# A token tower on one core: six gathered heads and two dense ones, replaced by eight dense heads

## The reference, cut to what matters

```
q = (x @ Wq).reshape(b, n, 8, 64) / 8
sim = einsum(x @ Wq_pk, pk_keys)              # 2 halves x 8 heads x 64 keys
scores, idx = top_k(sim, 16)                  # of each half
final, pk_idx = top_k(scores0[i] + scores1[j], 16)
kv_scores = softmax(final); ind = idx0 + 64 * idx1 + 4096 * head
k = sum over the 16 picks of kv_scores * keys_table[ind]
v = sum over the 16 picks of kv_scores * values_table[ind]
out = causal softmax(q k^T) v, heads joined, @ Wo
```

## Time and profile before

| what | value |
|---|---|
| median of 2 runs | 8935.81 us (8913.85 to 8957.77) |
| span of the profiled execution | 8919.9 us |
| granted TensorE clock, mean | 0.660 |
| PE, PEld busy | 65%, 43% |
| DVE, ACT, POOL busy | 36%, 23%, 49% |
| software DMA (the gathers) | 144384 packets, 295.20 MB |

### The profile page before, as it was taken

How to read it: one execution, slowest core, us unless ns; L and a number is a source line. 1 busy time by engine, 2 the same in 40 slices (tenths; PEclk the granted TensorE clock), 3 DMA queues, 4 the chain that set the end, 5 groups by cost and what they waited for, 6 DMA issues and landing times.

```text
span 8919.9 us, 86784 instructions
## 1 busy us (share of the span) xinstructions
PE 5811.1 (65%) x23616; PEld 3849.5 (43%) x23616; DVE 3250.8 (36%) x14095; ACT 2088.5 (23%) x4517; POOL 4374.7 (49%) x4574
## 2 busy tenths in 40 slices
PE   1367576575766757676665767667576666757677
PEld 1244444353444534444443544445344443534443
DVE  4334242433423243342424334232433423243036
ACT  0112122121322213132221312222131222222143
POOL 3454545545454554545455454545545445554500
PEclk9567566666756667675666667566666756666577
DMA  1111111111111111111111111111111111111100
GB/s 41 51 41 32 39 34 37 44 31 39 30 40 35 39 41 32 41 31 41 35 38 42 32 40 32 39 35 40 40 31 39 33 36 38 39 36 32 41 12 14
DMA packets 166480, 321.90 MB, mean 36 GB/s; under 512 B 82044, under 2 KB 90836, under 8 KB 165774
## 3 DMA queue, kind: packets, MB, share of 16 engines
q0 software_dynamic: 144384, 295.20, 12.5%
q1 hardware_dynamic: 21230, 20.00, 0.8%
q10 hardware_dynamic: 288, 0.07, 0.0%
HBM read 310.37 MB, written 4.61 MB: 35 GB/s over the span
## 4 chain that ended last, share of the span: by engine, by line
PE 36%; another core or an unknown queue 25%; issue 20%; DVE 14%; ACT 5%; DVEq 0%; ACTq 0%; DMA 0%; SPq 0%
PE gath L615 7%; PE accu L477 5%; PE dense L469 4%; PE work L668 2%; PE dense L464 2%; PE sims L662 2%; ACT past L902 2%; PE dense L470 1%; PE work L643 1%; PE work L698 1%; PE work L544 1%; PE work L655 1%; DVE front L1244 1%; DVE i L1243 1%
## 5 line engine op out<-in xcount | busy, mean ns | idle before, releaser
L429 POOL DMA_INDIRECT store<-in,idx_now x4512 | 4358.2, 966 | 3970.7 <-PE gath L615 2195.0
L615 PEld LDWEIGHTS gath<-wbd,store 128*128 128x128 f32 (+1 forms) x9024 | 1607.2, 266 | 783.7 <-issue 747.5
L615 PE MATMUL gath<-wbd,store 128*128 128x8 f32 (+1 forms) x9024 | 1553.7, 304 | 551.5 <-issue 432.8
L469 PE MATMUL dense<-parts_f,hot 128*128 128x375 bf16 x3072 | 905.0, 416 | 495.3 <-issue 420.7
L477 PE MATMUL accu<-dense_w,store 128*128 128x375 f32 x2048 | 1123.8, 640 | 11.9 <-issue 10.1
L902 ACT ACTIVATE past<-dense,edge 128x375 bf16<-128x375 f32 x1024 | 587.0, 573 | 2176.3 <-remote 1338.9
L464 PE MATMUL dense<-ranksT,hot 128*128 128x375 bf16 x1008 | 407.8, 405 | 847.1 <-ACT past L902 678.7
L469 PEld LDWEIGHTS dense<-parts_f,hot 128*128 128x128 bf16 x3072 | 322.2, 114 | 894.0 <-issue 820.6
L910 ACT ACTIVATE dense_w<-dense 128x375 f32<-128x375 f32 x1024 | 493.8, 482 | 887.3 <-remote 547.3
L464 PEld LDWEIGHTS dense<-ranksT,hot 128*128 128x128 bf16 x1008 | 158.4, 157 | 1083.0 <-issue 1033.7
L477 PEld LDWEIGHTS accu<-dense_w,store 128*128 128x128 f32 x2048 | 500.1, 258 | 142.2 <-issue 107.6
(11 more groups left out here) (285 smaller groups left out, 6983.9 us busy)
## 6 DMA issues: line engine op xcount, KB each, us to landing
store<-in,idx_now POOLq DMA_INDIRECT x4512
x_in<-in SPq DMA_DIRECT2D x16, 187.5 KB
store<-in SPq DMA_DIRECT2D x1, 2048.0 KB, 8.7
queries_kept<-n3T SPq DMA_DIRECT2D x16, 93.8 KB
h_saved<-h SPq DMA_DIRECT2D x16, 93.8 KB
store<-queries_kept SPq DMA_DIRECT2D x16, 93.8 KB, 2.4
store<-h_saved SPq DMA_DIRECT2D x16, 93.8 KB
out<-store SPq DMA_DIRECT2D x16, 93.8 KB
```

Of the source, the lines that this page charges most:

```text
L429: nc.gpsimd.indirect_dma_start(rows[0:slots, r * PER + i, :], None, kv_table, bass.IndirectOffsetOnAxis(ap=idx_now[0:slots, at:at + 1], ax ...
L469: mm(dense[:, 1, 0:S], hot[:, c, :], parts[:, k, h, :], start=(k == 0), stop=False)
L615: last = mm(gath[:, 0, at:at + 8], rows[0:slots, r * PER + i, :], wbd[0:slots, t * GATHERS + n, :], start=True, stop=True)
```

## The change

All eight heads are dense, and no step needs a gather. The weight of a row (i0, i1) is a product of two factors: exp of key i0's score against the maximum (`firsts`), and the same for i1 over the sum (`seconds`, as three bf16 parts, 32 of the 64 keys a group). What is new or different:

- A batch has 256 steps in 260 slots. The slot j holds, on TensorE: spread(j-2) (the constant `spread` brings the second factor to the 128 rows, `far` subtracts 1024 past), in every second of the first 56 slots one of the factors of a later head, accu(j-4), and coded(j) once past(j-1) is there. One PSUM bank holds `coded`, two take spreads and factors in turn; an item waits until the one two before it is taken.
- Of spread(i) with i even, ScalarE makes the Relu `shown` and GpSimd multiplies it by the first factor (`weigh` on GpSimd). With i odd VectorE does both in one instruction out of PSUM (`weigh` on VectorE), in its own stream between picks.
- The tables are streamed each batch: 32 pieces of 512 KB in a ring of 4, on SP's queue, ahead of that batch's `keep` and load of x.
- VectorE's picks lose row numbers, `places`, and the candidate indices; the codes are made for 8 heads by products and reductions over 2048 elements, the run comparison over 2048 too, and there are a difference over 1024 and the parts of the second factor. A tile has 23 pieces.
- Attention takes 88 slots (`STEPS_A`, `STEPS_B`: 14 or 15 a head for six heads, none for the last two), and the value matmuls of the last three heads move into its heads 4 to 6.

```diff
-FILL_FIRST = ((5, 2), (3, 2))
-FILL_SECOND = ((11, 6), (7, 4))
-FIRST_HEAD, STEPS_A, STEPS_B = 2, (1, 1, 1, 1, 1, 1, 0, 0), (2, 2, 2, 2, 2, 2, 0, 0)
+STEPS = H * CHUNKS
+SPREAD_LAG, SUM_LAG = 2, 4
+PREPARED_EVERY = 2
+FILL_PREPARE = (4, 3, 3, 3, 4, 4, 4, 4, 3)
+FILL_GRADIENT = (6, 6, 6, 6, 6)
+PICKS_GRADIENT = (2, 2, 1, 1, 1)
+FILL_FIRST = (8, 32)
+FILL_SECOND = (36, 34)
+FIRST_HEAD, STEPS_A, STEPS_B = 2, (8, 8, 8, 8, 8, 8, 0, 0), (6, 6, 6, 6, 7, 7, 0, 0)
+PICKS_INSIDE = (3, 3, 3, 3, 3, 3, 1, 1)
+PIECES_A, PIECES_B = 9, 14
+BY_VECTOR = frozenset(range(1, STEPS, 2))
...
+            def load_pieces(b):
+                for n in range(PIECES):
+                    sp.wait_ge(s["piece_out"], b * PIECES + n + 1)
+                    nc.sync.dma_start(table[:, n % PIECE_RING].rearrange("p c d -> p (c d)"), kv_table[n]).then_inc(piece_in[n % PIECE_RING], 16)
...
-                            nc.gpsimd.indirect_dma_start(
-                                rows[0:slots, r * PER + i, :], None, kv_table,
+                pool.wait_ge(s["taken"], b * ORDER.by_scalar + ORDER.taken_by_scalar[ORDER.spread[i]])
+                nc.gpsimd.tensor_tensor(dense_w[:, i % 3, :], shown[:, i % 3, :], first_of[:, i // CHUNKS, :],
+                                        ALU.mult).then_inc(s["weighed"], 1)
...
+            def dense_slot(b, j):
+                i = j - SPREAD_LAG
+                if 0 <= i < STEPS:
...
+                    to = bank_free(b, ORDER.spread[i])
+                    mm(to[:, 0:S], spread[0:3 * I1S, c % (CHUNKS // GROUPS), :], second_of[0:3 * I1S, c // (CHUNKS // GROUPS), h, :],
+                       start=True, stop=False)
+                    mm(to[:, 0:S], far[:], past[:, i % 2, :], start=False, stop=True).then_inc(s["spread"], 1)
+                if ORDER.factor_at(j) is not None:
+                    factor(b, *ORDER.factor_at(j))
+                i = j - SUM_LAG
+                if 0 <= i < STEPS:
...
+                    if i in BY_VECTOR:
+                        pe.wait_ge(s["by_vector"], b * ORDER.by_vector + ORDER.taken_by_vector[ORDER.spread[i]])
+                    else:
+                        pe.wait_ge(s["weighed"], b * WEIGHED[STEPS] + WEIGHED[i + 1])
+                    last = mm(accu[:, 0, 0:S], table[:, n % PIECE_RING, i % PIECE, :], dense_w[:, i % 3, :],
+                              start=(c == 0), stop=(c == CHUNKS - 1))
+                if j < STEPS:
+                    if j >= 1:
+                        pe.wait_ge(s["past"], b * STEPS + j)
+                    mm(coded, hot[:, j % CHUNKS, :], ranksT[:, j // CHUNKS, :], start=True, stop=True).then_inc(s["coded"], 1)
...
+            def weigh(b, i):
+                n = ORDER.spread[i]
+                dve.wait_ge(s["spread"], b * ORDER.items + n + 1)
+                v.scalar_tensor_tensor(dense_w[:, i % 3, :], dense[:, n % 2, 0:S], 0.0, first_of[:, i // CHUNKS, :],
+                                       ALU.max, ALU.mult).then_inc(s["by_vector"], 1)
...
+            def pick_among(picking, n, b, slots):
+                for k in range(n):
+                    next(picking, None)
+                    fill(b, slots * (k + 1) // n - slots * k // n)
```

More of the change, by code:

```diff
@@ L39 @@
 STARTS = OFFS + [TAIL_AT + i for i in range(K - K // 2)]
[L40 to L53, removed]
-CHUNKS = NKV // 128
-STEPS = HD * CHUNKS
+LATE = 3
+CHUNKS = NKV // 128
+STEPS = H * CHUNKS
+SPREAD_LAG, SUM_LAG = 2, 4
@@ L69 @@
+ORDER = Schedule()
+WEIGHED = [sum(1 for i in range(n) if i not in BY_VECTOR) for n in range(STEPS + 1)]
 HID, E = 256, 8
@@ new lines, in fill, with bank_free @@
+            def fill(b, n):
+                for j in range(slot[0], slot[0] + n):
+                    dense_slot(b, j)
+                slot[0] = (slot[0] + n) % SLOTS
+            def bank_free(b, n):
+                if n >= 2:
+                    if ORDER.of_vector[n - 2]:
+                        pe.wait_ge(s["by_vector"], b * ORDER.by_vector + ORDER.taken_by_vector[n - 2])
+                    else:
+                        pe.wait_ge(s["taken"], b * ORDER.by_scalar + ORDER.taken_by_scalar[n - 2])
+                return dense[:, n % 2]
@@ new lines, in factor @@
+            def factor(b, h, k):
+                to = bank_free(b, ORDER.factor[h, k])
+                for t in range(NT):
+                    if k == 0:
+                        last = tr(to[:, tile(t)], ranks[:, t, h, :], ident[0:P, 0:P])
+                    elif k == 1:
+                        for half in (slice(0, SUB), slice(SUB, 128)):
+                            last = mm(to[half, tile(t)], firsts[:, t, h, :], ident[0:P, 0:P], start=True, stop=True)
+                    else:
+                        last = mm(to[0:3 * I1S, tile(t)], seconds[:, t, h, k - 2].rearrange("p j i -> p (j i)"), ident_b[:],
+                                  start=True, stop=True)
+                last.then_inc(s["spread"], 1)
@@ L928, in middle_part, with fill, keep_factor @@
-            def middle_part(b):
-                act.wait_ge(s["part_rem"], b + 1)
-                nc.scalar.copy(parts[:, 1], dense_w[:]).then_inc(s["part_mid"], 1)
+            slot = [0]
+            def fill(b, n):
+                for j in range(slot[0], slot[0] + n):
+                    dense_slot(b, j)
+                slot[0] = (slot[0] + n) % SLOTS
+            def keep_factor(b, h, k):
+                n = ORDER.factor[h, k]
+                act.wait_ge(s["spread"], b * ORDER.items + n + 1)
+                src = dense[:, n % 2, 0:S]
+                if k == 0:
+                    last = nc.scalar.copy(ranksT[:, h, :], src)
+                elif k == 1:
+                    last = nc.scalar.copy(first_of[:, h, :], src)
+                else:
+                    last = nc.scalar.copy(second_of[0:3 * I1S, k - 2, h, :], src[0:3 * I1S])
+                last.then_inc(s["taken"], 1)
```

714 lines of the change are left out of this document (285 added, 429 removed).

## The result

The changed kernel takes 9370 us (two runs, 9368 and 9372) against 8936: a ratio of 1.047, 95% interval [1.041, 1.053], slower. The forecast was 9200.

What follows compares the result with a forecast made beforehand. No engine was taken as full: nearly half the chain was gather landings and late instructions. Start 739, fourteen rounds 7511, last round 435 and 496 behind sum to 9181; with 16 above the span 9197, say 9200 us; range 8450 to 9900.

Steps and rivals of the forecast that it cites:

- Start: Time before the first attention: counted from the first dense step at 368 in the old trace, 739 us, as now.
- Slot: One dense step in the slot loop: 1.16 us through the single code bank, just above TensorE's own 1.10.
- GpSimd's product: GpSimd's two-input product of 375 elements: taken as 0.9 us between 0.4 and 1.6, hidden in two slots of 2.32.
- VectorE's pieces: Picks on VectorE: 4.87 us for a head's codes, 73 us a tile, 0.60 for each product.
- TensorE can run ahead two slots: Behind each piece of picks on VectorE: TensorE gets 2.3 us ahead less the spread, 2.0, then waits.
- Stages: One round summed by stage: attention 183, turn 12, prepare 73, gradient 68, first fill 75.5, second 115; in all 536.5 us.
- last round: The round before the last attention, without following picks: 435 us.
- Rival 1: Whole loop: TensorE alone bounds and pieces of picks hide; 481 to 490 us a round, about 8500 us; chance 0.20.
- Rival 2: Slots: GpSimd's path sets them, product 1.6 us, 9900 us; or exclusion with VectorE at t=2, 9450; chance 0.13.
- Rival 3: Stages behind the turn and gradient: lower clock stays, 62 slots at 2.19 us, +64 a round, 10,100 us; chance 0.10.
- Rival 4: TensorE's slots: instructions still come late, +50 us a round, 9900 us; chance 0.12, half of it milder, near 9500.
- the unknown queue: 25% of the old kernel's chain: read as landings of 4512 indirect gathers of 0.966 us on GpSimd.

Runs made afterwards that it cites:

- e5: The kernel before, unchanged, profiled on another chip: 6375 us.
- e9: Changed kernel with a second GpSimd product of 160 elements before each of GpSimd's products: 9469 us, 1.0% more.
- e1: Changed kernel with every step's product made by ScalarE and GpSimd, none by VectorE: 8087 us.
- e7: e1 with the picked codes of all three tiles in SBUF, where e1 has two tiles' in PSUM: 8340 us, 3.1% above e1.
- e8: Changed kernel with VectorE making only the odd steps 1 to 29, in prepare, GpSimd the rest: 8238 us, 0.914 of the kernel before.

## Why the prediction was right, point by point

The mechanism held: pieces of picks on VectorE hold up its products, and TensorE with them. The total, 9181 for 9366, is in part luck, the sum of two errors of opposite sign: 173 us too much for the start, 358 too little for the rounds. With the start right and all else as it stands the forecast would have been 9024 us, 1% slower, and would not have been told from no change.

- **Start: wrong.** 739 was forecast, 565.9 measured. I counted from the first dense step at 368 of the earlier trace rows, and took off too little of the wait for the first gathers: that step stood behind gathers and late instructions (on the other chip, in e5, it comes at 251). Three tiles of 73 us from 55 on end at 274, and the factors do begin at 275.4, not at 423. The tile was right, the place from which I counted was not: that is 148 of the 173 us. The other 25 lie behind it, where 316 us were forecast and 290.5 measured.
- **Slot: right.** Coded matmuls lie 1.16 or 1.17 us apart where nothing else stands between (1.16 forecast).
- **GpSimd's product: right, with some luck.** 0.965 us (0.9). The rows left 0.4 to 1.6, and the reason for 0.9, that the memset's size is nearer, holds for the ratio alone (in elements the copy's 94 is nearer to 375 than 764). The path behind it was given too little room: "beyond 1.0 every 0.1 lengthens two slots by 0.1" would have made e9 9850; it took 9469. Factors and pieces stretch most pairs of slots.
- **VectorE's pieces: right.** Two operations of 2.28 us, and 5.50 with a product where 4.87 + 0.6 was forecast. "TensorE can run ahead two slots" is what the timeline shows.
- **Stages.** Turn 11.8 (12), prepare 72.2 (73), gradient 71.0 (68), second fill with the similarities 118 (120), last round 430 (435), the end 501 (496): right. Attention 204.6 (183) and first fill 85.6 (75.5): too low, and with them the round, 562.1 for 536.5, 358 us in 14. In attention the start took 20 us (15.3), at a granted clock of 0.50; the four heads with short pieces 97.0 (88.4); the two with long ones 34.0 and 34.3 (28.5 each); the end 19.4 (22). From the waits of one of these heads, 4646.4 to 4680.6 (us in total, times, longest):

```profile
PE dense L503 <- DVE dense_w L1110: 6.8, 2, 4.8
ACT kvT L887 <- PE accu L520: 6.3, 1, 6.3
```

TensorE stood twice behind VectorE's product, once for 4.8 us where I had allowed 2.0 a piece, and the sum of a head (L520) came 6.3 us after ScalarE was ready to copy it. How the missing 6 us a head divide among such waits was not tried by itself; with no product on VectorE (e1) the same heads take 26.6 us.

In the first fill the codes of the eight heads took 45.8 us (4883.4 to 4929.2), as forecast; the 10 us that I gave too little lie in the other 39.8, with the short pieces and the exponentials. There ScalarE loads a table (1.28 us) and makes three exponentials between two Relus, and TensorE stood 2.0 us for it.
- **Rival 1 (TensorE alone bounds, 8500): off, but its number was near.** e1 is the kernel in which it nearly holds (TensorE 418 of 475 us busy): 475.3 us a round against the 481 to 490 forecast.
- **Rival 2:** the lock was real (e7) and small: in the changed kernel it holds up single products at t=2 by up to 1.1 us, and by 1.6 beside the run comparison (one of 2.48 us at 4591.67); the longer path is e9.
- **Rival 3 (clock):** 0.83 to 0.94 in the stages with slots, where the earlier trace rows have 0.56 to 0.68 behind the turn; no stage stayed low. 5 us a round was given. How much it was is not known; e1's two fill stages at 1.00 show that it came with VectorE's waits.
- **Rival 4 (late instructions):** 9% of the chain and no 0.7 us spacing. From the earlier trace rows this was read rightly; that the lateness belongs to some chips only could not be seen in one trace. The reading of the unknown queue as gather landings was wrong (above), but no term of the sum rests on it. The 517.2 us a round that the forecast is set against were a mean with a short round in it; against the 523.9 of a full round, 536.5 was 13 us more.

What the change does by itself is therefore two things. On a chip with late instructions it removes most of them, and pays with VectorE's pieces: 5% slower. On the others there was little to remove: TensorE is busy for 300 us in the stages of the round at 3049.4 in e5's profile (350 of its 362 us), against 447 after, and the change costs 47%. e1, the best dense form that was run, is 14% below the changed kernel. It was not run beside a kernel before at 9000; against the 8936 of the first runs it would be 0.905, an estimate, which e8's 0.914 bears out, and beside one at 6375 it is 1.27.

## What to carry to other kernels

Totals per engine (342 of VectorE beside 393 of TensorE) do not say that two engines fit beside each other: with two buffers between them, the longest piece that one engine does in between decides, so move short urgent work off an engine that has long pieces, or cut the pieces. When the forecast for an early stage is derived from the old trace, count from the event that really releases it. Before a large rewrite against late instructions, profile the old kernel on a second chip.

## What the runs showed of the hardware

- The same program took 6375 us on some chips and 8936 to 9002 on others, at equal cost of a gather (0.97 us), of VectorE's long operations (1.82 us for 1600 elements on both) and of ScalarE's Relu (0.57). TensorE's matmuls took longer at the lower granted clock (0.66 against 0.74). The difference that stands out was time before instructions that could have begun: 1.4 us instead of 0.12 on VectorE, and over 4.4 us instead of 0.13 before a tenth of ScalarE's Relus. It came about 15 us after the first gather and went 10 us after the last one. The program without gathers took 9370 to 9382 us on either kind.
- A GpSimd product of 128x375 in f32 with both inputs in SBUF took 0.85 or 0.98 us undisturbed, and one of 160 columns 0.55. The Trainium skill (GPSIMD Engine Reference, "Elementwise — side-by-side cycle accounting") gives about 2.6 cycles an element. For 375 elements that is 0.81 us at 1.2 GHz, and 0.87 with the 0.06 us by which its 4497 ns for 2048 elements exceed the same rule (estimates); the total agrees with the trace. The slope does not: e9's 0.552 us for 160 elements and 0.937 for 375 give 1.8 ns an element, 2.1 cycles.
- A GpSimd product that began inside a VectorE operation of 2.28 us with two SBUF inputs ended 0.7 to 0.84 us after that one's end, 76 times of 76; beside the same operation reading one input from PSUM none took over 0.99, and beside VectorE's reductions of the same length, 256 times, none over 0.98. The Trainium skill (SBUF — State Buffer, "Who interferes with whom") states that such a pair contends and that the one that issues first holds the shared ports for its whole instruction; the traces and e7 agree.
